# A four-layer graph-attention kernel: the products of layer 0's heads in two column tiles of 64 weights

## The reference, cut to what matters

```python
Wh = (h @ W).reshape(B, N, 4, 64)
e = leaky_relu(s_src[:, :, None, :] + s_dst[:, None, :, :])   # slope 0.2
e = where(adj != 0, e, -inf)
alpha = softmax(e, axis=2)
h_out = einsum('bijh,bjhd->bihd', alpha, Wh)                  # per head: 512x512 times 512x64
x = x + elu(h_out)
```

## Time and profile before

| | |
|---|---|
| Time, median of 2 runs | 3085.64 us (3085.54 to 3085.74) |
| The profiled execution | 3088.44 us, its span 3086.6 us |
| TensorE busy, matmuls | 3027.8 us (98% of the span) |
| TensorE busy, weight loads | 2830.1 us (92%) |
| VectorE busy | 2453.4 us (79%) |
| ScalarE busy | 2321.4 us (75%) |
| GpSimd busy | 205.2 us (7%) |
| Mean granted TensorE clock | 0.996 of full speed |

### The profile page before, as it was taken

The page is one execution under the profiler, slowest core; times in us unless marked ns, Lnnn a source line. Parts: engine busy times, 40 slices in busy tenths (PEclk is TensorE's granted clock), DMA queues, the critical chain, the costliest instruction groups (busy, mean ns, idle before and its releaser), DMA issues.

```text
span 3086.6 us, 58782 instructions
## 1 busy us (share of the span) xinstructions
PE 3027.8 (98%) x21528; PEld 2830.1 (92%) x21528; DVE 2453.4 (79%) x7049; ACT 2321.4 (75%) x6303; POOL 205.2 (7%) x410
## 2 busy tenths in 40 slices
PE   8999999999999999999999999999999999999998
PEld 7899999999999999999999999999999998999987
DVE  6878787887887888878878888888778787787866
ACT  6677777777778777778787787777787777877776
POOL 2000000000000000000000000000000000000000
PEclk9999999999999999999999999999999999999998
DMA  2000000000000000000000000000000000000000
GB/s 76 1 22 1 15 15 15 15 1 15 15 15 15 15 1 15 15 15 15 2 14 15 15 15 15 1 15 15 15 15 8 8 15 15 15 15 1 1 1 28
DMA packets 16336, 41.54 MB, mean 13 GB/s; under 512 B 5297, under 2 KB 6833, under 8 KB 16049
## 3 DMA queue, kind: packets, MB, share of 16 engines
q1 hardware_dynamic: 16048, 37.77, 3.5%
HBM read 20.99 MB, written 16.78 MB: 12 GB/s over the span
## 4 chain that ended last, share of the span: by engine, by line
PE 82%; ACT 9%; DVE 7%; issue 1%; POOL 1%; SPq 0%; DMA 0%; DVEq 0%; ACTq 0%
PE bank L516 45%; PE bank L585 14%; PE bank L620 14%; ACT Z L1044 4%; PE bank L573 4%; PE bank L537 2%; DVE R L792 2%; PE bank L671 2%; PE bank L561 1%; DVE x L1009 1%; DVE Z L1006 1%; ACT Z L1196 1%; ACT Z L1202 1%; ACT Z L1191 1%; ACT Z L1021 1%
## 5 line engine op out<-in xcount | busy, mean ns | idle before, releaser
L585 PE MATMUL bank<-hw,R 128*128 128x257 f32 x3072 | 707.4, 383 | 0.5 <-DVE R L792 0.5
L585 PEld LDWEIGHTS bank<-hw,R 128*128 128x128 f32 x3072 | 569.0, 191 | 75.5 <-ACT hw L1082 1.5
L620 PEld LDWEIGHTS bank<-hw,R 128*128 128x128 f32 x4096 | 490.9, 192 | 5.5 <-DVE hw L825 1.2
L620 PE MATMUL bank<-hw,R 128*128 128x65 f32 x4096 | 494.8, 270 | 0.8 <-DVE R L792 0.8
L792 DVE SCALAR_TENSOR_TENSOR R<-bank,E,mask_ne 128x512 f32<-128x512 f32 x640 | 450.5, 743 | 13.4 <-PE bank L573 12.5
L1044 ACT ACTIVATE Z<-x,nm,rs 128x256 f32<-128x256 f32 x512 | 283.2, 593 | 52.3 <-DVE x L1009 32.2
L1247 POOL TENSOR_TENSOR rs<-ve,mhalf 128x4 f32<-128x4 f32 x128 | 134.5, 1051 | 2825.7 <-DVE ve L744 2159.2
L516 PE MATMUL bank<-wfc_hi,oThi 128*128 128x256 f32 (+1 forms) x1024 | 302.0, 295 | 2.1 <-DVE oTlo L871 1.9
L516 PE MATMUL bank<-wfc_hi,oTlo 128*128 128x256 f32 (+1 forms) x1024 | 289.7, 283 | 0.0
L516 PE MATMUL bank<-wfc_lo,oThi 128*128 128x256 f32 (+1 forms) x1024 | 289.7, 283 | 0.0
L1067 ACT COPY Z<-bank 128x258 f32<-128x258 f32 (+1 forms) x512 | 183.1, 369 | 93.3 <-PE bank L516 93.0
(11 more groups left out here) (262 smaller groups left out, 8353.9 us busy)
## 6 DMA issues: line engine op xcount, KB each, us to landing
x<-in_x_dram SPq DMA_DIRECT2D x32, 512.0 KB, 3.4
out_dram<-x SPq DMA_DIRECT2D x32, 512.0 KB, 2.6
R<-in_adj_dram SPq DMA_DIRECT2D x2, 512.0 KB, 7.3
Z<-in_L_gnn_mlp_w_dram SPq DMA_DIRECT2D x2, 512.0 KB, 5.4
O<-in_L_gnn_W_fc_dram SPq DMA_DIRECT2D x1, 1024.0 KB, 6.7
R<-in_L_gnn_W_dram SPq DMA_DIRECT2D x1, 256.0 KB, 3.7
R<-in_L_gnn_W_hand_dram SPq DMA_DIRECT2D x1, 256.0 KB, 6.7
rowt<-in_L_gnn_W_dram SPq DMA_DIRECT2D x1, 256.0 KB, 4.7
```

Of the source, the lines that this page charges most:

```text
L585: ins = e.matmul(bk[:, 0:257], P[:, j, i * 128:(i + 1) * 128], hw[:, j, 0:257], start=(j == 0), stop=(j == NBLK - 1))
L620: ins = e.matmul(bk[:, i * 66:i * 66 + 65], P[:, (4 * h + j) % PTILES, i * 128:(i + 1) * 128], hv[:, j, h, 0:65], start=(j == 0 and i == 0 ...
```

## The change

Each call of line 620 is replaced by two. The first takes 64 of the 128 columns of the square of P as its weights and writes partitions 0 to 63 of the bank, the second takes the other 64 and writes partitions 64 to 127. The tile position, (0, 0) or (0, 64), is given with each. The moving operand, the results' places, the waits and the semaphore steps are as before.

```diff
                     for i in range(NBLK):
-                        ins = e.matmul(bk[:, i * 66:i * 66 + 65], P[:, (4 * h + j) % PTILES, i * 128:(i + 1) * 128],
-                                       hv[:, j, h, 0:65], start=(j == 0 and i == 0), stop=(j == NBLK - 1),
-                                       skip_group_check=True)
+                        for c in range(0, 128, 64):
+                            ins = e.matmul(bk[c:c + 64, i * 66:i * 66 + 65],
+                                           P[:, (4 * h + j) % PTILES, i * 128 + c:i * 128 + c + 64], hv[:, j, h, 0:65],
+                                           start=(j == 0 and i == 0), stop=(j == NBLK - 1), skip_group_check=True,
+                                           tile_position=(0, c))
                     ins.then_inc(up("att0", b))
```

## The result

The change takes 3039.69 us (3037.82 to 3041.55) against 3085.64 us before, 46 us less. The ratio is 0.9851 with a 95% interval of 0.9809 to 0.9893. Timed again beside the first experiments, it took 3040.03 us against 3088.70, ratio 0.9843 (0.9828 to 0.9857). The forecast was 3137, slower by 1.7%. The direction was wrong.

The account below looks back on a forecast made before the run. TensorE was taken to bound the kernel, with weight loads setting line 620's price: 457 us removed, 508 added, switches 0, so 3085.6 + 51 = 3137 us (+1.7%). The forecast case's range was 3085 to 3170, the wide range 2930 to 3290.

Parts of the forecast that it names:

- What bounds the kernel: Whole kernel: TensorE, with matmuls in flight 98% of the span; time added at line 620 goes into the total nearly one for one.
- The load sets the price, 0.112 us: Line 620: loading 128 weights, not streaming 65 columns (0.055 us), sets each pair's price; 4,096 x 0.112 = 457 us.
- the price for nearly equal load and stream: New pairs of line 620: 6 ns added to each load of 0.056 us (bounds 0 and 7), making 0.062 us.
- if the two tiles take turns: Line 620's new pairs: assumed the tiles don't overlap, so 8,192 x 0.062 = 508 us, 51 us more than 457.
- the rival: Line 620, faster: the tiles work side by side, 0.031 us a pair, about 2923 us in total; chance 0.32.
- the order of the passes: Line 620: both passes of one half precede the other's, so a waiting second pass may block what follows; argued against overlap.
- when the switches take most of the gain: Side-by-side tiles at line 620, with switch costs leaving the total within 2% of before; chance 0.05 of that rival's 0.32.
- The switches: Between whole-array products and line 620's column tiles: 780 switches, taken to cost 0.
- The other end: Upper bound for switches around line 620: the array empties each time, 780 x 0.165 = 129 us; waiting loads add 66 us.
- second rival: Around line 620's rows, slower: the array empties at each switch, 3266 us, or 3332 with loads behind it; chance 0.25.
- The first rival's sum: Line 620 with overlapping tiles: 254 us, 203 less, a fifth kept by other engines: about 2923 us; 3016 with switches priced.
- "The semaphores ... unchanged": Whole kernel: semaphores, waits, VectorE's and ScalarE's instructions and DMAs unchanged; TensorE's own waits stay near today's, the largest 10.3 us.

Follow-up runs that it names:

- the first experiments: On the change, timed in one group with its repeat: halves apart, 3129.8 us; column sums later, 3034.8 us; two blocks j a turn, 3064.0 us.
- e7: The change with both halves of the weights put into one column tile a turn (a timing alone, the result differs): 3203.0 us, ratio 1.0375.
- e1: The change with all four blocks of the lower half first, then all four of the upper, in each turn: 3129.8 us, ratio 1.0135.
- e10: The change with blocks 0 and 2 of each turn done by the whole array, 1 and 3 in two column tiles: 3336.7 us, ratio 1.0809.

## Why the prediction was wrong, by its steps

**What bounds the kernel: right.** TensorE did, and the time followed line 620 (one tile: 51 us more within rows, 116 in all).

**The load sets the price, 0.112 us: right.** So were its halves: in one tile a pair takes 0.058 us, beside 0.056 by proportion and 0.062 with the price for nearly equal load and stream. Of the 6 ns 2 were there. (4,096 x 0.112 is 459 and not 457 us, so the 51 us more would be 49; nothing hangs on it.)

**The step that failed is "if the two tiles take turns".** The sum of the forecast rests on it. No row could show it, and I held the order of the passes against the rival: "the second pass of the upper half must wait for the first, and anything kept in order behind it waits too". The pairs stand 0.029 us apart (the rival had 0.031), and e7 shows that this is the second tile. Its chance of 0.32 should have been the highest. That the time still came within 2% is the case of this rival that had 0.05, "when the switches take most of the gain": two errors stood against one another, and the 97 us between forecast and result measure neither. The Trainium skill, "TensorEngine Tiling (Array Packing)", section "Key Properties", says that tiles load and multiply in parallel; the trace agrees, 0.007 us between the starts of two pairs. The prediction cited the rule and still put a guess about order above it. The guess was not empty, as e1 shows: had the loops stood the other way round, 90 us would have been lost and the change would have been slower.

**The switches: taken at 0, and they cost.** The other end was 780 x 0.165 = 129 us, or 0.33 us a row. The single starts give 0.24 us for a row in and out, with 363 rows 87 us, and 0.324 with the overlap that the rows had before, 118 us. (The 390 rows came from a miscount: the chain from 1000 us has ten rows with 88 pairs, not eleven with 96, which gives 384; the trace has 363.) A price of the second rival's kind was thus there together with the first rival's gain. The Trainium skill, "TensorEngine Tiling (Array Packing)", section "Key Properties", says that changing the tiling mode drains TensorE. The first load of a row comes only 0.20 us or more behind the last matmul ahead, and that agrees with it, though the runs don't show what exactly is waited for.

**The first rival's sum.** 203 us less, of which a fifth was to be kept by others, gives 2923; the 3016 "with the price of the switches" doesn't follow from it, 2923 + 129 is 3052. That is near to what was measured, 3040, and the terms close: 457 - 8,192 x 0.029 = 219 us gained, 118 lost at the rows (0.324 each), 27 more in the wait for `hsr`, 13 in the distances of the other lines, and about 11 in further waits next to the rows. That leaves 50 us, and 46 to 51 are seen. No term of the prediction had the overlap: before, the second start came 0.065 us after the first in the earlier trace rows, not 0.112, and that cover, 0.08 us a row or 29 us in all, is gone.

**"The semaphores ... unchanged", waits "near today's": wrong.** Rows of four turns, 3.52 us, now have their loads in 1.95, and VectorE doesn't deliver `hsr` earlier for that; with one tile, where such rows are long again, the wait is 3.0 us as before. What stood behind them, `sums(0)`, came 1.0 us too early in nearly each batch.

## What to carry to other kernels

Where TensorE is bound by weight loads with few moving columns, two column tiles can halve the price of a square of weights (0.112 to 0.058 us a pass here), but let the calls of the two tiles alternate: all of one and then all of the other lost 90 us here. Count the switches between tiled and whole products first. A row of tiles lost 0.32 us here and a pair of 128 weights gains 0.054, so a row of fewer than six such pairs would lose, and the usual row of eight kept 0.11 of its 0.43 us. Once a line gets faster in an order that is written out by hand, look at what stands behind it: the next wait takes its share, and moving one step only moves it on.

## What the runs showed of the hardware that was not expected

In e10, where whole and tiled products alternate within a turn, TensorE's mean granted clock was 0.974, against 0.993 to 0.998 in every other run. A row of four such turns began at 1052.13 and had matmuls in flight until 1057.6, with nothing waited for. At its beginning the clock was 1.00 (2.4 GHz), and before its end it had fallen to 0.50, the 1.2 GHz level. Behind it the products of line 516 came 0.21 us apart instead of 0.119. Two stretches, and the matmuls:

```profile
1052.00:1056.00 4.00, 4.00 (x41) 3.18 (x39) 3.50 (x13) 3.73 (x11) 0.00 (x0) 1.00 0.00 0
1056.30:1057.60 1.30, 1.30 (x11) 0.94 (x11) 0.00 (x0) 0.00 (x0) 0.00 (x0) 0.50 0.05 13
```

```profile
1052.13 5.52 PE L622 MATMUL bank<-hw,R 128*128 128x65 f32 x48
1057.58 0.58 PE L516 MATMUL bank<-wha_hi,hsr 128*128 128x256 f32 x1
1057.96 0.42 PE L516 MATMUL bank<-wha_lo,hsr 128*128 128x256 f32 x1
1058.17 0.63 PE L516 MATMUL bank<-wha_hi,hsr 128*128 128x256 f32 x2
```

All 17 falls of the clock between 200 and 2800 us of this trace come during a row of four turns or within 0.2 us of its end, but not every such row has one: over the whole trace 21 of 33. Why is not shown.

With 65 columns one pair, a load of 64 weights and its stream, keeps a tile for 0.058 us, and load and stream are nearly equal in it. So neither half the columns (0.058) nor four tiles (0.055) shortened a step much by itself; both together did (0.031).
